# A hybrid mixer and FFN kernel: low parts of the shared expert by GpSimd, no queue drain in the FFN blocks, and the second mixer's first norm computed at the end of FFN 1

## What is computed

```
x = x + MixerA(LN(x));  x = x + FFN(LN(x));  x = x + MixerB(LN(x));  x = x + FFN(LN(x))

MixerA(u): u + out_proj(selective_scan(silu(conv(in_proj(rmsnorm(u))))) * silu(z))
MixerB(u): h = u + out_proj(rmsnorm(state_scan(silu(conv(in_proj(rmsnorm(u) * norm_w)))) * silu(z)))
           h + down(silu(gate(rmsnorm(h))) * up(rmsnorm(h)))
FFN(u):    SwiGLU_shared(u) + sum over the 2 chosen of 8 experts of weight * SwiGLU_e(u)
           weights: softmax of the logits, top 2, normalised;  SwiGLU: down(silu(gate) * up), 938 wide
```

## Time and profile before

| | before |
|---|---|
| median of 3 runs | 1072.92 us |
| the profiled execution's own time | 1073.7 us |
| its span, first to last instruction | 1071.9 us |
| mean granted clock of TensorE | 0.963 |
| TensorE matmul busy | 973.5 us (91%) |
| TensorE weight load busy (beside the matmuls) | 685.5 us (64%) |
| VectorE busy | 741.6 us (69%) |
| ScalarE busy | 601.2 us (56%) |
| GpSimd busy | 594.4 us (55%) |

### The profile page before, as it was taken

The page is one execution under the profiler, slowest core; times in us unless marked ns, Lnnn a source line. Parts: engine busy times, 40 slices in busy tenths (PEclk is TensorE's granted clock), DMA queues, the critical chain, the costliest instruction groups (busy, mean ns, idle before and its releaser), DMA issues. The chain is left out here.

```text
span 1071.9 us, 16173 instructions
## 1 busy us (share of the span) xinstructions
PE 973.5 (91%) x4707; PEld 685.5 (64%) x4707; DVE 741.6 (69%) x1197; ACT 601.2 (56%) x1129; POOL 594.4 (55%) x465
## 2 busy tenths in 40 slices
PE   5899989888899899999997869887899899999997
PEld 2323333233466799999995436645567699999996
DVE  3899999999488466666665687645478566666665
ACT  5576566765643455555553876576742455555553
POOL 1389797999510888538612737530110788635732
PEclk8999989999999999999999889988999999999999
DMA  4222223343411134211103000000421233212104
GB/s 145 50 71 73 82 67 91 79 107 89 157 53 56 36 93 122 71 57 34 49 13 97 27 0 2 1 1 0 149 62 33 51 91 88 60 57 72 53 26 123
DMA packets 60399, 69.40 MB, mean 65 GB/s; under 512 B 6232, under 2 KB 42848, under 8 KB 60320
## 3 DMA queue, kind: packets, MB, share of 16 engines
q1 hardware_dynamic: 55328, 58.15, 18.7%
q0 software_dynamic: 4992, 10.23, 3.9%
HBM read 57.74 MB, written 10.62 MB: 64 GB/s over the span
## 5 line engine op out<-in xcount | busy, mean ns | idle before, releaser
L764 POOL TENSOR_TENSOR a_hc<-a_h,a_c_sb 128x512 f32<-128x512 f32 x128 | 159.5, 1268 | 40.3 <-DVE a_h L672 40.3
L449 PE MATMUL ps<-a_hc,eye 128*128 128x512 f32 x256 | 134.1, 640 | 8.6 <-POOL a_hc L764 7.6
L589 ACT ACTIVATE ps<-a_delta,a_neg_a 128x512 f32<-128x512 f32 x128 | 87.3, 687 | 64.8 <-DVE a_h L672 64.3
L449 PEld LDWEIGHTS ps<-a_hc,eye 128*128 128x128 f32 x256 | 45.7, 196 | 76.2 <-issue 40.0
L672 DVE TENSOR_TENSOR_SCAN a_h<-ps,a_state,a_b_u 128x512 f32<-128x512 f32 x64 | 78.6, 1263 | 3.1 <-ACT ps L589 2.1
L672 DVE TENSOR_TENSOR_SCAN a_h<-ps,a_b_u 128x512 f32<-128x512 f32 x64 | 75.2, 1206 | 4.2 <-ACT ps L589 4.0
L1126 PE MATMUL ps<-g_ring_rounded,g_q_hi_rounded 128*128 x312 | 77.0, 337 | 0.0
L1126 PE MATMUL ps<-f_ring_rounded,f_q_hi_rounded 128*128 x312 | 77.0, 337 | 0.0
L995 POOL DMA_INDIRECT g_rows<-xn_rows,g_source x39 | 37.0, 949 | 62.5 <-DVE g_source L1520 51.4
L995 POOL DMA_INDIRECT f_rows<-xn_rows,f_source x39 | 37.4, 960 | 58.0 <-DVE f_source L1520 46.9
L652 DVE TENSOR_TENSOR a_b_u<-a_du,ps 128x1024 f32<-128x1024 f32 x57 | 68.0, 1192 | 0.1
(11 more groups left out here) (483 smaller groups left out, 2810.0 us busy)
## 6 DMA issues: line engine op xcount, KB each, us to landing
a_c_sb<-c_rows SPq DMA_DIRECT2D x64, 256.0 KB, 3.3
f_ring<-in_gu SPq DMA_DIRECT2D x16, 469.0 KB, 4.6
g_ring<-in_gu SPq DMA_DIRECT2D x16, 469.0 KB, 4.3
f_ring<-in_dn SPq DMA_DIRECT2D x8, 512.0 KB, 5.9
g_ring<-in_dn SPq DMA_DIRECT2D x8, 512.0 KB, 5.8
xn_rows<-f_work SPq DMA_DIRECT2D x8, 256.0 KB, 3.6
f_rows<-token_rows SPq DMA_DIRECT2D x8, 256.0 KB, 5.1
xn_rows<-g_work SPq DMA_DIRECT2D x8, 256.0 KB, 2.8
```

Of the source, the lines that this page charges most:

```text
L449: nc.tensor.matmul(ps[:, Y + f, :], k.eye[:, :], hc[:, s % WAITING, :], start=False, stop=(n == NST - 1)).then_inc(y_added, 1)
L589: nc.scalar.activation(ps[:, A + m % NA, :], delta[:, f, cols(g)], ACT.Exp, scale=neg_a[:, f, n:n + 1])\
L764: nc.gpsimd.tensor_tensor(hc[:, m % WAITING, :], h[:, s % DEPTH, :], c_sb[:, i % RING, :], ALU.mult)\
```

## The change

In both FFNs, tiles 0 to 18 of the shared expert's down product go over to the split form with three fp32r matmuls. For tiles 0 to 20 (`EARLY` = 21) VectorE's product goes to a buffer of its own in SBUF, ScalarE makes the high part from it one tile later, and GpSimd the low part (`low_part(q)`), which `down(q)` waits for. Tiles 19 and 20 had their low parts from VectorE. The splitting of expert 1 is divided into five parts, `split_parts`, one behind each third low part (q = 2, 5, 8, 11, 14). The plain weights are no longer loaded. The FFN blocks end with no drain of GpSimd's queue.

FFN 1 gets a tail (`following`). Behind the turning of its last rows TensorE centres x and makes the variances of mixer B's first norm, each chunk when its last add to x is done; ScalarE squares and takes the joint logarithms into a buffer that outlives the block; VectorE copies the centred x to `xn`. SyncE loads three of mixer B's weights at the end of FFN 1 and waits for them there.

Mixer B starts with four Exps on the joint logarithms, VectorE copies two variances to SBUF (`keep_variance`), scales the input weights and the four chunks from PSUM, and copies the other two variances. The plain logarithm is one Ln of 128x2048 with the softplus; its Exps follow in chunks 0 to 3 of the state scan, and GpSimd scales the residual there, a chunk of 512 in each. Two projections wait for the variances to be copied, since they use the same banks of PSUM.

```diff
-def ffn_stage(k, d, which, tag, cleared, ready, out=None, logs=None):
+def ffn_stage(k, d, which, tag, cleared, ready, out=None, logs=None, following=None):
...
-    PLAIN, COUNT, FIND, SOURCES = 19, 7, 20, 22
+    EARLY, COUNT, FIND, SOURCES = 21, 7, 20, 22
     done = 0 if logs is not None else ready
     def pace(q):
-        return 0 if q <= 3 else 5 if q < 9 else 1 if q < PLAIN else 3
-
-    plain_dn = prods[:, 1, :].rearrange("p (i m) -> p i m", i=TILES)
+        return 0 if q <= 3 else 5 if q < 9 else 1 if q < 19 else 3
...
     def split(n):
-        return max(0, n - PLAIN)
+        return max(0, n - EARLY)
...
-    with stage, nc.Block() as block:
+    with stage, nc.Block(no_gpsimd_drain=True) as block:
...
-            sp.dma_start(plain_dn[:, :, :], d["dn"][0, :, :].rearrange("(i p) m -> p i m", p=P)).then_inc(plain_loaded, 16)
...
+            if following is not None:
+                sp.dma_start(following.w_in[:, :], d["w_inB"]).then_inc(next_loaded, 16)
+                sp.dma_start(following.head_rows[:, :, :].rearrange("p a b -> p (a b)"), d["headsB"].partition_broadcast(P))\
+                    .then_inc(next_loaded, 16)
+                sp.dma_start(following.w_out[:, :, :], d["w_outB"]).then_inc(next_loaded, 16)
+                sp.wait_ge(next_loaded, 48)
...
+            def split_parts(n):
                 place = (n - 1) % RING
                 high, low, dn = ring[:, place, 0:GW], ring[:, place, GW:2 * GW], down_of(ring, place)
                 raw, raw_dn = raw_ring[:, place, GW:2 * GW], down_of(raw_ring, place)
                 pool.wait_ge(w_loaded[place], 48 * ((n - 1) // RING + 1))
                 nc.gpsimd.tensor_copy(high, raw).then_inc(w_high, 1)
+                yield
                 nc.gpsimd.tensor_copy(dn[:, :, 0, :], raw_dn[:, :, 1, :]).then_inc(w_high, 1)
+                yield
                 pool.wait_ge(w_high, 2 * n - 1)
-                nc.gpsimd.tensor_tensor(low, raw, high.bitcast(F32), ALU.subtract)
+                for part in (slice(0, INTER), slice(INTER, GW)):
+                    nc.gpsimd.tensor_tensor(low[:, part], raw[:, part], high[:, part].bitcast(F32), ALU.subtract)
+                    yield
                 pool.wait_ge(w_high, 2 * n)
                 nc.gpsimd.tensor_tensor(dn[:, :, 1, :], raw_dn[:, :, 1, :], dn[:, :, 0, :].bitcast(F32),
                                         ALU.subtract).then_inc(w_ready, 1)
-
-            split_expert(1)
+                yield
+
+            def split_expert(n):
+                for _ in split_parts(n):
+                    pass
+
+            def low_part(q):
+                m = k_of(q % TILES)
+                pool.wait_ge(high_ready, q + 1)
+                nc.gpsimd.tensor_tensor(p_at(q_lo, q, m), p_at(norm_rs, q, m), p_at(q_hi, q, m).bitcast(F32),
+                                        ALU.subtract).then_inc(low_by_pool, 1)
+
+            first = split_parts(1)
+            for q in range(EARLY):
+                low_part(q)
+                if q % 3 == 2:
+                    next(first, None)
...
-                if q < PLAIN:
-                    pe.wait_ge(prod_done, q + 1)
-                    nc.tensor.matmul(ps[:, SUMS[c], :], plain_dn[:, i, :], p_at(norm_sq, q, P),
-                                     start=(i == 0), stop=(i == TILES - 1)).then_inc(summed, 1)
-                    return
-                pe.wait_ge(low_ready, split(q + 1))
+                if q < EARLY:
+                    pe.wait_ge(low_by_pool, q + 1)
+                else:
+                    pe.wait_ge(low_ready, split(q + 1))
...
-            pe.wait_ge(plain_loaded, 16)
...
+            if following is not None:
+
+                def centre_next(c):
+                    pe.wait_ge(out_added, c + 1)
+                    nc.tensor.matmul(ps[:, NEXT_CENT[c], :], k.cent[:, :], k.x[:, cols(c)], start=True, stop=True)\
+                        .then_inc(next_centred, 1)
+
+                def variance_next(c):
+                    pe.wait_ge(next_squared, c + 1)
+                    nc.tensor.matmul(ps[:, NEXT_VAR[c], :], k.ones[:, :], work[:, cols(c)], start=True, stop=True)\
+                        .then_inc(next_var, 1)
+
+                centre_next(0)
+                centre_next(1)
+                variance_next(0)
+                centre_next(2)
+                variance_next(1)
+                centre_next(3)
+                variance_next(2)
+                variance_next(3)
...
-                nc.scalar.activation(p_at(q_hi, q, m), up_at(q, m), ACT.Copy).then_inc(high_ready, 1)
+                nc.scalar.activation(p_at(q_hi, q, m), p_at(norm_rs, q, m) if q < EARLY else up_at(q, m), ACT.Copy)\
+                    .then_inc(high_ready, 1)
...
-                if q > PLAIN:
+                if q:
...
+            if following is not None:
+
+                def square_next(c):
+                    act.wait_ge(next_centred, c + 1)
+                    nc.scalar.activation(work[:, cols(c)], ps[:, NEXT_CENT[c], :], ACT.Square).then_inc(next_squared, 1)
+
+                def log_next(c):
+                    act.wait_ge(next_var, c + 1)
+                    nc.scalar.activation(following.joint[:, cols(c)], ps[:, NEXT_VAR[c], :], ACT.Ln, bias=k.eps[:, 2:3])
+
+                nc.scalar.preload_act_table_set("natural_log")
+                square_next(0)
+                square_next(1)
+                log_next(0)
+                square_next(2)
+                log_next(1)
+                square_next(3)
+                log_next(2)
+                log_next(3)
...
-                if 4 <= q < PLAIN:
+                if 4 <= q < EARLY:
                     dve.wait_ge(summed, q - 3)
-                to = p_at(norm_sq, q, m) if q < PLAIN else up_at(q, m)
+                to = p_at(norm_rs, q, m) if q < EARLY else up_at(q, m)
...
-                if q > PLAIN:
+                if q > EARLY:
...
-            dve.wait_ge(summed, PLAIN)
...
+            if following is not None:
+
+                def keep_centred(c):
+                    dve.wait_ge(next_squared, c + 1)
+                    nc.vector.tensor_copy(k.xn[:, cols(c)], ps[:, NEXT_CENT[c], :])
+
+                for c in range(NCH):
+                    keep_centred(c)
...
+class Given:
+
+    def __init__(self, k, ctx):
+        sb = lambda name, shape: k.sb("b_" + name, shape, F32, ctx=ctx)
+        self.joint = sb("xp", [P, T])
+        self.w_in, self.w_out = sb("w_in", [P, 2 * DI + 2 * P + 4]), sb("w_out", [P, FT, P])
+        self.head_rows = sb("head_rows", [P, 2, 4])
...
-    norm = Norm(k, "nb", sem, sq_at=lambda c: bc[:, 1, cols(c)], joint_at=lambda c: y[:, 0, cols(c)],
-                plain_at=lambda c: y[:, 1, cols(c)], place=lambda c: xp[:, cols(c)], small=k.eps[:, 2:3])
...
+                    pe.wait_ge(scaled, NCH if i == 1 else c + 1)
+                    if i == 2:
+                        pe.wait_ge(var_kept, NCH)
...
-            norm.of_tensor(pe)
...
+                act.wait_ge(normed, g + 1)
...
-            norm.of_scalar(act)
-            act.wait_ge(loaded, 48)
+            for c in range(NCH):
+                nc.scalar.activation(xp[:, cols(c)], xp[:, cols(c)], ACT.Exp, scale=-0.5).then_inc(joint_ready, 1)
...
+            act.wait_ge(var_kept, NCH)
+            nc.scalar.activation(rms[:, :, :], rms[:, :, :], ACT.Ln, bias=k.eps[:, 0:1]).then_inc(plain_log, 1)
...
+                if c < NCH:
+                    act.wait_ge(plain_log, 1)
+                    nc.scalar.activation(rms[:, c, :], rms[:, c, :], ACT.Exp, scale=-0.5).then_inc(plain_ready, 1)
...
-            norm.of_pool(pool)
...
+                if c < NCH:
+                    pool.wait_ge(plain_ready, c + 1)
+                    nc.gpsimd.tensor_tensor(k.xn[:, cols(c)], k.xn[:, cols(c)], rms[:, c, :], ALU.mult).then_inc(normed, 1)
...
-            norm.keep_centred(dve)
-            dve.wait_ge(loaded, 48)
+            def keep_variance(c):
+                nc.vector.tensor_copy(rms[:, c, :], ps[:, VAR[c], :]).then_inc(var_kept, 1)
+
+            keep_variance(1)
+            keep_variance(2)
             nc.vector.tensor_scalar(w_in[:, :], w_in[:, :], k.vec[:, VB_NORM:VB_NORM + 1], (1.0 + 1e-6) ** -0.5,
                                     ALU.mult, ALU.mult).then_inc(weighed, 1)
-            norm.scale(dve)
+            for c in range(NCH):
+                dve.wait_ge(joint_ready, c + 1)
+                nc.vector.tensor_tensor(xp[:, cols(c)], ps[:, CENT[c], :], xp[:, cols(c)], ALU.mult).then_inc(scaled, 1)
+            keep_variance(0)
+            keep_variance(3)
...
+            dve.wait_ge(normed, NCH)
...
+        logs = k.sb("logs", [P, 2, CH])
+        between = ExitStack()
+        given = Given(k, between)
+        f_counters, f_spent = ffn_stage(k, d, 0, "f", a_spent, NCH - 1, following=given)
         a_counters.close()
-        logs = k.sb("logs", [P, 2, CH])
-        mixer_b_stage(k, d, f_spent, logs)
+        mixer_b_stage(k, d, f_spent, logs, given)
```

(8 more changed lines are left out.)

33 lines of the change are left out of this document (15 added, 18 removed).

## The result

The changed kernel takes **1098.51 us** (median of 4 runs, 1092.79 to 1102.67) against 1072.79 for the kernel before (4 runs, 1072.53 to 1074.78): a ratio of 1.0233, 95% interval 1.0204 to 1.0261. It is slower, as forecast (1090.5), by 25.7 us where 17.6 were forecast. That is the upper end of the range (1098): the median is half a microsecond over it, the ratio (1.0233 of 1072.8 is 1097.8) just inside. Its profiled execution took 1098.48 us, with a span of 1096.2 and a mean granted clock of 0.962.

A forecast was written before the change was run, and what follows sets the result against it. VectorE, as much as TensorE, was taken to bound the path up to `find_tokens`. 1073.7 - 9.1 - 0.65 + 0.9 + 27 - 0.6 = 1091.3 us profiled, 0.8 above the median: 1090.5 us; range 1058 to 1098.

The forecast's parts named there:

- the port: FFNs' routing: GpSimd reading SBUF and VectorE reading two SBUF operands exclude each other for the whole instruction; +13.5 us an FFN.
- Rival (b): FFNs' routing: turns cost little, small operations slip in between, TensorE hides the rest; 1061 us in all, chance 29%.
- The walk: FFNs' routing, tile by tile in program order: GpSimd's reads and VectorE's steps taking turns lengthen an FFN by 16.8 us.
- bound of 40 us: FFNs, `product(4)` to last routing operation: both engines' port uses end to end, all else hidden; against 34.6, +4 an FFN.
- Products 4 to 9: FFNs, tiles 4 to 8: low parts stop small routing steps, and splitting pieces add more; +8.9 us on 11.45.
- From there to the last routing operation: FFNs, tiles 9 to 19: large routing operations alternate with low parts and splitting pieces; about 32 us against 23.2.
- The start: Start of the first FFN: L1343 no longer waits for L977, so the exponentials come some 1.4 us sooner.
- TensorE's 3.0 us: FFNs' shared expert: the split down product saves 0.16 us a tile, 3.0 an FFN, worth only 0.3.
- Part 2: Mixer B's start: with the norm moved into FFN 1's tail, the first convolution comes 9.1 us sooner.
- case of a high clock: Mixer B's start: if TensorE is at its high clock, VectorE's queue ends last; gain 9.1 to 9.9 us.
- The drain: Removing GpSimd's queue drain gains 0.65 us at the kernel's end and adds nothing at mixer B's start.
- The chunks: Mixer B, chunks 0 to 3: one more GpSimd multiplication of 1.27 us each; +0.9 us (0 to 1.8).

The follow-up runs named there:

- One tile more of patience: The changed kernel with each early down product one tile later on TensorE (behind gate and up of q+3 instead of q+2); ratio 1.0159 to the kernel before.
- e_memset_whole: The changed kernel with GpSimd's low parts replaced by memsets (taken as zero) and expert 1's splitting in one piece; ratio 0.9965 to the kernel before.
- e_tail: The kernel before with mixer B's norm moved into FFN 1's tail and the residual's logarithm with the softplus, GpSimd's drain kept; ratio 0.9902 to the kernel before.
- e_tail_nodrain: The changed kernel with the FFNs' shared expert as before: norm in FFN 1's tail, no drain; ratio 0.9906 to the kernel before, 0.9922 measured again.
- e_low_memset: The changed kernel with each GpSimd low part replaced by two memsets (taken as zero), splitting still in five parts; ratio 0.9981 to the kernel before, 1071.3 us.

## Why the prediction was right, and where it wasn't

**What bounds the kernel, and the port.** Right, and shown. Reads by GpSimd that nobody waits for cost 17 us of the kernel's time, writes nothing; with writes in place of the low parts' reads the changed kernel is 27 us faster, and in VectorE's steps nearly all of FFN 2's loss stands (15.4 of 15.6 us). Rival (b), that the small operations slip in between, falls: in proportion they suffer most, from 0.29 to 1.15 us.

**The size.** The walk gave +16.8 us for an FFN, and I took +13.5, as a value between the walk and a bound of 40 us for perfectly packed turns. That discount is the step that failed: measured are +17.2 and +16.3. (The bound takes a turn as 10 to 15% shorter than its record, for which the prediction shows no row. The traces bear it out: an operation that stood ends 0.14 us less than its own length behind the end of the other, as L1343 in the earlier trace rows (0.54 for 0.68 us) and L1522 above (1.38 for 1.52).) That the walk's total was met is in part luck, for its parts were off in opposite ways. Products 4 to 9: +5.4 (FFN 2 +6.8), forecast +8.9, since not each low part meets a small step. From there to the last routing operation: +13.1 (+8.8), forecast +8.7. The start: -1.3 (+0.7), forecast -1.4 for the first FFN; in the second no L1343 waits long for L977, so it had nothing to gain. With this gain the working isn't at one: the walk takes off 0.8 us from 17.6, the lower bound the whole 1.4 in both FFNs.

**What the sum had no term for.** TensorE waits for the held low parts (9.8 us in FFN 1, 6.5 in FFN 2) and its clock falls: +2.5 us behind the routing in FFN 1. The unused subtractions (+5.0) and the parts of the splitting (+5.3), less the split product's gain (1.3), make 9.0 of the 18.5 / 15.6 us of added routing time. The remaining 9.5 / 6.6 are in neither of them. The loop from VectorE's turns to the low parts, to TensorE, to the next product and back to VectorE would show as VectorE's idle time: 6.1 us more than before in FFN 1, but 0.5 in FFN 2. The rest is steps that stand longer than in the two kernels together (12.4 / 15.4 us against 5.4 and 5.0). One tile more of patience gives back 3.9 / 2.5 us. How much of the longer standing is due to the 21 instead of 16 operations, to their longer records (1.28 against 1.04 us) and to which engine is issued first is open; no kernel here tells these apart.

**Scatter.** The changed kernel scatters by 10 us (1092.8 to 1102.7, granted clock 0.972 to 0.958), the one before by 2 there, and by 5 and 8 on the two other chips with times near 1073. That the bound of +17 us for an FFN was also the top of the range left no room for the clock.

**TensorE's 3.0 us.** Counted as 0.3, because VectorE holds the path. Without the reads, 1.3 us an FFN appear in the routing time (e_memset_whole).

**Part 2.** Forecast -9.1, measured -9.0, step by step as in the traces above; the table load that the earlier trace rows show between logarithm and Exp is there again at 608.77. It does not speak against a set of tables with both functions: both kernels load the set `natural_log` by its name before the logarithms, and another set was not tried. TensorE was at its lower level again for most of the first products (1.06 us each for the two in the middle, before and after), so the case of a high clock did not come.

**The drain.** -0.65 forecast, -0.6 in the two profiles. So small a term isn't shown by them alone: from the last add to the end the kernels without the drain take 2.6 to 3.6 us, those with it 3.2 to 5.1. It is worth nothing that can be seen at the boundary once Part 2 is there (e_tail against e_tail_nodrain: 0.9902 and 0.9906).

**The chunks.** Forecast +0.9, measured -0.6. GpSimd's period does grow from 3.2 to 3.8 us, and the fifth chunk starts 1.9 us later than before, seen from the first convolution. But the gating behind the fourth takes it all up (the sixth is 0.1 later); the 0.6 comes later, where the granted clock is 0.95 in place of 0.89 (63 us).

## What to carry to other kernels

Before work is handed to GpSimd because it is idle, look at what VectorE reads meanwhile: if VectorE's operations have two inputs in SBUF and GpSimd's work reads SBUF, the two take turns, and where VectorE is nearly full, as here, the work can cost more there than where it came from (1.0233 against 1.018). Ask also who waits for the engine that loses its turns: unused reads cost 5 us of routing time here, low parts in a chain, with the splitting between them, 15.6 to 18.5. And when the walk through the program's order is the only working made from this code, don't shade it towards a perfect packing that nothing in the code brings about.

## What the hardware showed

- GpSimd's memset of SBUF runs beside a VectorE operation with two SBUF inputs at no cost to either (0.85 us, and 1.22 as before); its copy and its subtraction do not.
- The loser of a turn isn't fixed, and isn't told by size: the operation that comes second stands. A small VectorE step lost 2.0 us (0.19 to 2.16, e_low_memset), a large one 1.7 (1.22 to 2.92, at 339.47 in the changed kernel), and behind large ones GpSimd's subtraction took 1.8 to 2.3 us for 1.04.
- The same kernel took 1073 us on one chip and 1204 on another, with waits of up to 12.8 us in the routed experts that no event on the core ends in the profile. The parts added up on it to what the first chip showed for the whole, by ratios (1.0230 against 1.0233) as well as by differences of medians (+35.0 and -11.1 against +25.7 us); which of the two carries over is not shown. The routing time of the untouched FFN was the same, 34.6 us.
